# Two-layer cross-attention on one core: x and keys also loaded turned, their scalings spread over the partitions through DRAM, out0 and the residual left turned

## The reference, cut to what matters

```python
def layer0(x, c, f):                                   # out_a uses c, out_v uses f
    def cma(x, k):
        q = _ln(x) @ Wq + bq;  kk = _ln(k) @ Wk + bk;  v = _ln(k) @ Wv + bv
        return softmax(q @ kk.T * 128 ** -0.5) @ v @ Wo + bo
    res = cma(x, c) + cma(x, f) + x
    return _ln(res) @ fc_W + fc_b + res

def layer1(x1, c):
    Q = x1 @ Wq + bq;  K = c @ Wk + bk;  V = c @ Wv + bv
    return x1 + softmax(Q @ K.T * 128 ** -0.5) @ V @ Wo + bo
```

## Time and profile before

| | |
|---|---|
| time, median of 3 runs | 169.53 us (167.81 to 170.84) |
| profiled execution, first to last instruction | 167.2 us; the page lists no other time for it |
| TensorE busy | 155.5 us, 93% |
| VectorE busy | 131.4 us, 79% |
| ScalarE busy | 124.2 us, 74% |
| GpSimd busy | 76.4 us, 46% |
| moved by DMA | 15.93 MB |

### The profile page before, as it was taken

The page is one execution under the profiler, slowest core; times in us unless marked ns, Lnnn a source line. Parts: engine busy times, 40 slices in busy tenths (PEclk is TensorE's granted clock), DMA queues, the critical chain, the costliest instruction groups (busy, mean ns, idle before and its releaser), DMA issues.

```text
span 167.2 us, 6323 instructions
## 1 busy us (share of the span) xinstructions
PE 155.5 (93%) x2442; PEld 121.7 (73%) x2442; DVE 131.4 (79%) x400; ACT 124.2 (74%) x384; POOL 76.4 (46%) x104
## 2 busy tenths in 40 slices
PE   6799998999999999799999999989999999999682
PEld 6769674896689687767786787667788887995350
DVE  1693499999899789999999996497688997596531
ACT  3431559869988979599879788977978789866930
POOL 2026269789676523714979624194532022110210
PEclk9965579999999999999999999999999999999955
DMA  5999999900001010101010011001010100101113
GB/s 139 299 380 380 378 379 378 364 33 0 2 4 67 0 67 0 68 2 67 4 63 4 0 67 65 6 0 67 0 67 20 47 6 4 67 0 65 63 67 125
DMA packets 9982, 15.93 MB, mean 95 GB/s; under 512 B 1249, under 2 KB 3682, under 8 KB 9954
## 3 DMA queue, kind: packets, MB, share of 16 engines
q1 hardware_dynamic: 9522, 15.14, 25.1%
q10 hardware_dynamic: 432, 0.40, 1.0%
HBM read 11.35 MB, written 4.19 MB: 93 GB/s over the span
## 4 chain that ended last, share of the span: by engine, by line
PE 73%; DVE 9%; ACT 7%; issue 4%; DMA 3%; POOL 2%; ACTq 1%; POOLq 0%
PE ps L1526 9%; PE ps L1465 8%; PE ps L1508 7%; PE ps L1576 5%; PE ps L1516 5%; PE ps L1496 4%; PE ps L1541 4%; PE ps L1534 4%; PE ps L1485 4%; PE ps L1456 4%; PE ps L1475 4%; PE ps L1449 4%; DMA cf_sb<-in_cf 3%; PE ps L1568 3%; ACT exp L632 3%
## 5 line engine op out<-in xcount | busy, mean ns | idle before, releaser
L384 POOL TENSOR_TENSOR prob<-exp,rsum 128x512 f32<-128x512 f32 x16 | 16.7, 1042 | 23.5 <-DVE rsum L1025 23.5
L390 POOL TENSOR_TENSOR prob<-exp,rsum 128x256 f32<-128x256 f32 x16 | 9.8, 613 | 29.0 <-DVE rsum L1085 29.0
L356 POOL TENSOR_TENSOR z_sb<-x_sb,x_rstd 128x512 f32<-128x512 f32 x15 | 15.4, 1040 | 15.9 <-ACT x_rstd L543 14.1
L632 ACT ACTIVATE exp<-ps,exp_bias 128x64 f32<-128x64 f32 x64 | 19.2, 315 | 3.5 <-DVE exp_bias L1080 3.4
L1061 DVE SCALAR_TENSOR_TENSOR x_sb<-ps,res_rstd,res_sb 128x128 f32<-128x128 f32 x64 | 19.2, 342 | 0.2 <-issue 0.2
L1465 PE MATMUL ps<-zT_sb,m 128*128 128x512 f32 x32 | 17.8, 645 | 0.0
L1526 PE MATMUL ps<-wd,resT_sb 128*128 128x130 f32 x128 | 17.6, 280 | 0.0
L1508 PE MATMUL ps<-w,mix_sb 128*128 128x128 f32 x128 | 17.5, 280 | 0.0
L378 POOL TENSOR_TENSOR cfn_sb<-cf_scaled,cf_shift 128x512 f32<-128x512 f32 x15 | 15.6, 1042 | 4.0 <-issue 2.9
L1526 PEld LDWEIGHTS ps<-wd,resT_sb 128*128 128x128 f32 x128 | 15.6, 191 | 2.0 <-ACT resT_sb L609 1.5
L371 POOL TENSOR_TENSOR cf_scaled<-cf_sb,cf_rstd 128x512 f32<-128x512 f32 x15 | 15.4, 1043 | 2.7 <-ACT cf_rstd L555 2.5
(11 more groups left out here) (141 smaller groups left out, 384.2 us busy)
## 6 DMA issues: line engine op xcount, KB each, us to landing
x_sb<-in_x SPq DMA_DIRECT2D x16, 256.0 KB, 6.8
out<-out_sb SPq DMA_DIRECT2D x16, 256.0 KB, 2.0
cf_sb<-in_cf SPq DMA_DIRECT2D x15, 256.0 KB, 7.1
ct_sb<-in_ct SPq DMA_DIRECT2D x16, 128.0 KB, 7.9
...
cf_sb<-in_cf ACTq DMA_DIRECT2D x1, 256.0 KB, 4.9
...
```

Source lines behind the costliest of these rows:

```text
L356: pool.tensor_tensor(z_sb[:, g % Z_SLOTS, :, :], x_sb[:, g, :, :], wide_x(g), ALU.mult).then_inc(z_pool, 1)
L384: pool.tensor_tensor(prob0[:, g % PROB0_SLOTS, :, :, :], exp0[:, g % EXP0_SLOTS, :, :, :], wide0(rsum0, g), ALU.mult).then_inc(prob0_pool, 1)
L632: last = nc.scalar.activation(exp1[:, g % EXP1_SLOTS, p, :], ps[:, bank + u, v * S:(v + 1) * S], ACT.Exp, bias=exp1_bias[:, g, p:p + 1], a ...
```

## The change

- x is also loaded turned (xt: 128 features by 512 query columns) and, from group 4 on, both key sets too (kt). x, xt, cf, kt and ct no longer have a place for each group but 4, 8, 9, 3 and 6 slots, and SP waits for a slot to come free before it loads.
- Groups 0 to 3 (TURNED) still go by z, zT, copy_zT and cfT, copy_cfT. From group 4 on the scalings and shifts of a batch of two groups lie in 40 columns of `rows`; TensorE turns them (turn_rows), ScalarE copies them (copy_rowsT), SP stores them to DRAM (store_rows) and loads them back repeated over the partitions (spread_x, spread_k, spread_s, each 128 partitions by 1024 elements, 512 KB). GpSimd then multiplies or adds them (scale_xt, scale_kt, shift_kt), and t0 and s0 read the results. scale_cf stays for mix0, which now reads scaled keys without the shift.
- out0 is one matmul of 512 columns and its result is turned already. residual adds xt and a folded bias and writes resT_sb, which dense reads directly; resN turns it back for stats_res only, which reads PSUM. ScalarE scales dense's result (gain, four instructions), x1T turns it, x1 (VectorE) adds residual and bias in one instruction of 512 columns.
- The foldings of weights change a little (a bias as a column of the affine tile, bv and bo folded into out0's bias), `keep_busy` has 11 + 3 + 3 + 1 matmuls in place of 8, and the lists of all five engines are new.

```diff
-Z_SLOTS, ZT_SLOTS, CFS_SLOTS, CFN_SLOTS, CFT_SLOTS, T0_SLOTS, DIFF0_SLOTS = 3, 2, 2, 4, 2, 2, 2
-EXP0_SLOTS, PROB0_SLOTS, PROB0T_SLOTS, MIX0_SLOTS, RES_SLOTS, X1_SLOTS, REST_SLOTS = 2, 2, 2, 2, 4, 2, 2
+X_SLOTS, XT_SLOTS, CF_SLOTS, KT_SLOTS, CT_SLOTS, SPREAD_SLOTS = 4, 8, 9, 3, 6, 2
+Z_SLOTS, ZT_SLOTS, CFV_SLOTS, CFK_SLOTS, KS_SLOTS, CFT_SLOTS, T0_SLOTS, DIFF0_SLOTS = 2, 3, 4, 2, 2, 3, 2, 2
+EXP0_SLOTS, PROB0_SLOTS, PROB0T_SLOTS, MIX0_SLOTS, REST_SLOTS, GAIN_SLOTS = 2, 2, 2, 2, 4, 2
 X1T_SLOTS, T1_SLOTS, EXP1_SLOTS, PROB1_SLOTS, PROB1T_SLOTS, MIX1_SLOTS, OUT_SLOTS = 4, 2, 2, 2, 2, 2, 3
...
+TURNED = [0, 1, 2, 3]
+BATCHES = [[0], [1], [2, 3], [4, 5], [6, 7], [8, 9], [10, 11], [12, 13], [14, 15]]
+SPREAD_FROM = 3
...
+            def store_rows(b):
+                at = b - SPREAD_FROM
+                sp.wait_ge(rowsT_copied, at + 1)
+                sp.dma_start(rows_dram[at, :, :], rowsT[:, at % SPREAD_SLOTS, :]).then_inc(rows_stored[at % SPREAD_SLOTS], 16)
+
+            def spread_x(b):
+                at = b - SPREAD_FROM
+                sp.wait_ge(rows_stored[at % SPREAD_SLOTS], 16 * (at // SPREAD_SLOTS + 1))
+                if at >= SPREAD_SLOTS:
+                    sp.wait_ge(zT_scaled, BATCHES[b - SPREAD_SLOTS][-1] + 1 - len(TURNED))
+                sp.dma_start(x_spread[:, at % SPREAD_SLOTS, :, :].rearrange("p g t -> p (g t)"),
+                             rows_dram[at, 0:8, :].rearrange("r t -> (r t)").unsqueeze(0).broadcast_to([D, 8 * P])
+                             ).then_inc(x_spread_in[at % SPREAD_SLOTS], 16)
+
+            def spread_k(b):
+                at = b - SPREAD_FROM
+                sp.wait_ge(rows_stored[at % SPREAD_SLOTS], 16 * (at // SPREAD_SLOTS + 1))
+                if at >= SPREAD_SLOTS:
+                    sp.wait_ge(ks_done, BATCHES[b - SPREAD_SLOTS][-1] + 1 - len(TURNED))
+                sp.dma_start(k_spread[:, at % SPREAD_SLOTS, :, :].rearrange("p g t -> p (g t)"),
+                             rows_dram[at, 8:24, :].rearrange("(h r) t -> h (r t)", h=2).unsqueeze(1
+                             ).broadcast_to([2, C, 8 * P])).then_inc(k_spread_in[at % SPREAD_SLOTS], 16)
+
+            def spread_s(b):
+                at = b - SPREAD_FROM
+                sp.wait_ge(rows_stored[at % SPREAD_SLOTS], 16 * (at // SPREAD_SLOTS + 1))
+                if at >= SPREAD_SLOTS:
+                    sp.wait_ge(cfT_shifted, BATCHES[b - SPREAD_SLOTS][-1] + 1 - len(TURNED))
+                sp.dma_start(s_spread[:, at % SPREAD_SLOTS, :, :].rearrange("p g t -> p (g t)"),
+                             rows_dram[at, 24:40, :].rearrange("(h r) t -> h (r t)", h=2).unsqueeze(1
+                             ).broadcast_to([2, C, 8 * P])).then_inc(s_spread_in[at % SPREAD_SLOTS], 16)
...
+            def scale_xt(g):
+                slot, half = spread_at(g)
+                slot_in(pool, xt_in, g, XT_SLOTS)
+                spread_in(pool, x_spread_in, g)
+                need(pool, t0_made, g - ZT_SLOTS + 1)
+                pool.tensor_tensor(zT_sb[:, g % ZT_SLOTS, :], xt_sb[:, g % XT_SLOTS, :], x_spread[:, slot, half, :],
+                                   ALU.mult).then_inc(zT_scaled, 1)
+
+            def scale_kt(g):
+                slot, half = spread_at(g)
+                at = g - len(TURNED)
+                slot_in(pool, kt_in, g, KT_SLOTS, len(TURNED))
+                spread_in(pool, k_spread_in, g)
+                need(pool, cfT_shifted, at - KS_SLOTS + 1)
+                pool.tensor_tensor(blocks(ks_sb[:, g % KS_SLOTS, :]), kt_sb[:, at % KT_SLOTS, :, :, :, :],
+                                   blocks(k_spread[:, slot, half, :]), ALU.mult).then_inc(ks_done, 1)
+
+            def shift_kt(g):
+                slot, half = spread_at(g)
+                at = g - len(TURNED)
+                pool.wait_ge(ks_done, at + 1)
+                spread_in(pool, s_spread_in, g)
+                need(pool, s0_made, g - CFT_SLOTS + 1)
+                pool.tensor_tensor(cfT_sb[:, g % CFT_SLOTS, :, :, :, :], blocks(ks_sb[:, g % KS_SLOTS, :]),
+                                   blocks(s_spread[:, slot, half, :]), ALU.add).then_inc(cfT_shifted, 1)
...
+            def copy_rowsT(b, bank):
+                at = b - SPREAD_FROM
+                act.wait_ge(rowsT_made, at + 1)
+                if at >= SPREAD_SLOTS:
+                    act.wait_ge(rows_stored[at % SPREAD_SLOTS], 16 * (at // SPREAD_SLOTS))
+                nc.scalar.copy(rowsT[:, at % SPREAD_SLOTS, :], ps[0:40, bank, 0:P]).then_inc(rowsT_copied, 1)
...
-            def copy_resT(g, bank):
-                act.wait_ge(resT_made, g + 1)
-                need(act, dense_made, g - REST_SLOTS + 1)
-                nc.scalar.copy(resT_sb[:, g % REST_SLOTS, :], ps[:, bank, :]).then_inc(resT_copied, 1)
-
-            def copy_x1T(g, bank):
-                act.wait_ge(x1T_made, g + 1)
-                if g == 0:
-                    act.wait_ge(row_bias_done, 1)
-                need(act, final_done, g - X1T_SLOTS + 1)
-                nc.scalar.activation(x1T_sb[:, g % X1T_SLOTS, :], ps[:, bank, :], ACT.Identity, bias=row_bias[:, :]
-                                     ).then_inc(x1T_copied, 1)
+            def gain(g, bank):
+                act.wait_ge(dense_made, g + 1)
+                act.wait_ge(res_rstd_done, g + 1)
+                need(act, x1T_made, g - GAIN_SLOTS + 1)
+                for p in range(PAIRS):
+                    at = (p % 2) * (D + 2)
+                    last = nc.scalar.mul(gain_sb[:, g % GAIN_SLOTS, p, :], ps[:, bank + p // 2, at:at + D],
+                                         res_rstd[:, g, p // 2, p % 2:p % 2 + 1])
+                last.then_inc(gain_act, 1)
...
             def residual(g, bank):
                 dve.wait_ge(out0_made, g + 1)
-                need(dve, resT_made, g - RES_SLOTS + 1)
-                need(dve, x1_done, g - RES_SLOTS + 1)
-                v.tensor_tensor(res_sb[:, g % RES_SLOTS, :, :], by_pair(ps[:, bank, :]), x_sb[:, g, :, :], ALU.add
-                                ).then_inc(res_done, 1)
-
-            def stats_res(g):
-                dve.wait_ge(res_done, g + 1)
+                slot_in(dve, xt_in, g, XT_SLOTS)
+                if g == 0:
+                    dve.wait_ge(out0_bias_done, 1)
+                need(dve, resN_made, g - REST_SLOTS + 1)
+                need(dve, dense_made, g - REST_SLOTS + 1)
+                need(dve, x1T_done, g - REST_SLOTS + 1)
+                v.scalar_tensor_tensor(resT_sb[:, g % REST_SLOTS, :], ps[:, bank, :], out0_bias[:, 0:1],
+                                       xt_sb[:, g % XT_SLOTS, :], ALU.add, ALU.add).then_inc(res_done, 1)
+
+            def stats_res(g, bank):
+                dve.wait_ge(resN_made, g + 1)
                 for u in range(DUOS):
                     last = v.bn_stats(res_stats[:, g, u, :, :].rearrange("p v k -> p (v k)"),
-                                      res_sb[:, g % RES_SLOTS, 2 * u:2 * u + 2, :].rearrange("p v d -> p d v"))
+                                      ps[:, bank, 2 * u * P:2 * (u + 1) * P].rearrange("p (v d) -> p d v", v=2))
                 last.then_inc(res_stats_done, 1)
 
-            def x1(g, bank):
-                dve.wait_ge(dense_made, g + 1)
+            def key_biases(g, bank):
                 dve.wait_ge(res_rstd_done, g + 1)
-                need(dve, x1T_made, g - X1_SLOTS + 1)
...
+            def x1(g, bank):
+                dve.wait_ge(x1T_made, g + 1)
+                if g == 0:
+                    dve.wait_ge(row_bias_done, 1)
+                need(dve, t1_made, g - X1T_SLOTS + 1)
+                need(dve, final_done, g - X1T_SLOTS + 1)
+                v.scalar_tensor_tensor(x1T_sb[:, g % X1T_SLOTS, :], ps[:, bank, :], row_bias[:, 0:1],
+                                       resT_sb[:, g % REST_SLOTS, :], ALU.add, ALU.add).then_inc(x1T_done, 1)
 
...
+            def turn_rows(b, bank, *reads):
+                pe.wait_ge(x_rstd_done, b + 1)
+                pe.wait_ge(cf_shift_done, b + 1)
+                after(*reads)
+                nc.tensor.transpose(ps[0:40, bank, 0:P], rows[:, b, :], ident[:, :]).then_inc(rowsT_made, 1)
...
-                for u in range(DUOS):
-                    for v in range(2):
-                        p = 2 * u + v
-                        last = mm(ps[:, bank, p * P:(p + 1) * P], mix0_sb[:, g % MIX0_SLOTS, u, v, :, :], w01[:, 0:D],
-                                  start=True, stop=True)
-                last.then_inc(out0_made, 1)
-
-            def resT(g, bank, *reads):
+                mm(ps[:, bank, :], w01[:, 0:D], mix0_sb[:, g % MIX0_SLOTS, :, :, :, :], start=True, stop=True
+                   ).then_inc(out0_made, 1)
+
+            def resN(g, bank, *reads):
                 pe.wait_ge(res_done, g + 1)
                 after(*reads)
                 for p in range(PAIRS):
-                    last = nc.tensor.transpose(ps[:, bank, p * P:(p + 1) * P], res_sb[:, g % RES_SLOTS, p, :], ident[:, :])
```

(37 more changed lines are left out.)

1887 lines of the change are left out of this document (986 added, 901 removed).

## The result

The changed kernel takes **260.2 us**, median of four runs (257.6 to 261.6), against 169.7 us for the kernel before in four runs beside it: 1.533 times the time, 95% interval 1.517 to 1.548. The forecast was 248 us, from the case of two engines, whose own range was 226 to 272. Executions of one kernel can lie some per cent apart, so where the medians of two kernels are close their lowest runs are compared too. The profiled execution has a span of 259.3 us.

The account below looks back on a forecast made before the run. TensorE's instruction stream bounds the kernel before (93% of span); afterwards two DMA engines carrying the spreads: 35 + 132 + 8 + 18 + 12 + 2 + 5 + 34 = 246 us span, forecast 248 us, 8-in-10 range 163 to 272.

Parts of the forecast that it names:

- the case of two engines: spread_k and spread_s loads each move on only two of sixteen DMA engines: 248 us, own range 226 to 272, chance 0.70.
- The mechanism: In spread_k and spread_s, the source's slowest dimension counts 2, so two DMA engines each carry 256 KB and fourteen carry nothing.
- The size of a spread: One 512 KB spread_k or spread_s load on two engines at 23.75 GB/s each: 11.0 us, range 9.7 to 12.
- The low bound of 9.7 us: Shortest spread_k or spread_s load, its two engines undisturbed by the other fourteen; with all loads hidden, 226 us in total.
- The serial sum: Spreads and other loads queue on the two DMA engines as one serial resource: 246 us of span.
- the term of 12 us: Time the two DMA engines stand empty: waits at shifts(5) and store_rows(7), plus each batch's store and landing latency.
- TensorE: Its instruction stream: 13.4 us less transposes, 0.9 more small ones, 0.5 less out0, 1 more filler; 167.2 to 155.2 us.
- The other engines: Busy time of ScalarE 108 to 115 us, VectorE about 124, GpSimd 89, all beside TensorE and no bound.
- A: Rival: spreads go on many engines, round trip hidden, TensorE's saving holds: 159.5 us (153 to 164), chance 0.17.
- T: Length of one spread_k or spread_s load; a batch costs 2T + 1.4 + 5 us, fitting 15.9 us up to T = 4.7.
- B: Rival: many engines, but half the DRAM round trip shows, through SP's waits or late loads: 172 to 184 us, chance 0.13.
- the round trip of 8.5 us: A batch's scalings to DRAM and back with all sixteen engines sharing, inside 15.9 us of TensorE work per batch.

Follow-up runs that it names:

- The standalone loads: Separate SyncE-only kernel, one awaited 512 KB load at a time: source of 2 rows repeated 64 times 12.15 to 12.76 us, one row repeated 128 times 3.39 us.
- halves: Changed kernel with spread_k and spread_s each issued as two loads of one repeated row to 64 partitions: 173.9 us; run again 175.9 us, 1.029 times before.

## Why the prediction was right, step by step

**The mechanism** was the one named: the source's slowest dimension of two. It was argued from the code's two patterns and the durations of other transfers. The standalone loads (12.2 to 12.8 us against 3.4, with 0.13 of the engines busy) and halves (86 of 90 us) show it. GpSimd waited and TensorE was 62% busy, as said; but the DMA engines did not stay near 2/16 and 50 GB/s. In 40 to 60 and 100 to 120 us they were at 0.44 and 0.22, 134 and 75 GB/s, since the other loads run beside the spreads.

**The size of a spread** was taken as 11.0 us, and the first two are 10.9 us apart. The single one, waited for, is 12.2 to 12.8, which has the landing and the empty start in it. The low bound of 9.7 us has no row behind it; the quickest that two engines were seen to move is 51 GB/s, 10.3 us for 512 KB. The low end of the range does not come out of its own words either: 12 x 1.3 us less for the spreads and no 18 us for the loads give 248 - 34 = 214 us, not 226. The measured time lies at the other end, so nothing hung on it.

**The serial sum** was 35 + 132 + 8 + 18 + 12 + 2 + 5 + 34 = 246; the span is 259.3. The terms against the trace:

| term | predicted | in the trace |
|---|---|---|
| first spread issued | 35 | 30.8 |
| from there to the last landing | 172 | 187 (217.8 less 30.8) |
| from there to the end | 39 | 41.5 |

The first spread is 4 us early. The changed opening has the full clock from 10 to 20 us, and the kernel before with 14 filler matmuls shows that the filler brings 3.4 us of such a lead; it was priced at up to 4.8 us of cost and turned out a gain there. The chain of the kernel after has cfT(3) 4.6 us ahead of the earlier trace rows; the first out0 follows it:

```profile
26.33 0.59 PE ps L1679 x4
...
27.04 1.13 PE ps L1735 x2
```

The middle is the mis-sized step, by 15 us, and 11 of them lie in the term of 12 us for the time in which the two engines stand empty. The trace gives, from the use of a spread to the issue of the next: 85.0 to 91.7, 119.4 to 120.9, 149.4 to 162.3, and 190.5 to 192.6, 23 us in all, bounded by when GpSimd could use the landed rows. The longest is at the batch that the prediction named: k_spread(6) is used at 149.44, and store_rows(7) goes out at 158.58, 9.1 us later. But the way there is another. The prediction had store_rows(7) stand behind load_kt(13), which needs scale_kt(10); load_kt(13) went out at 150.72 already. The rows themselves came late: shifts(7) stands in GpSimd's list behind scale_kt(10) and (11), three other kinds of work and shift_kt(10), and runs at 156.70, though ScalarE's part of its inputs was there at 151.5; then come TensorE's turn at 157.97 and ScalarE's copy at 158.29. The prediction had named this kind of wait for shifts(5) and did not count it for batch 7. So of the sum the term for the empty engines was mis-sized, 12 us for 23, by the GpSimd work that stands between a landing and the next rows. That GpSimd work is a likely part of what made the kernel with one two-engine load a batch slower than expected, too.

**TensorE.** Four groups are still turned, 16 transposes each of zT and cfT. Where the long waits are gone, TensorE is busy for 146.8 us (halves) and 144.0 us (without the later spreads; 145.8 in its second run), 9 to 12 us under before; predicted were 12 less (155.2 against 167.2 of span). Part of it is the clock of the opening: before with 14 filler matmuls has 152.9 us, 2.6 less than before. The filler takes 6.7 us in halves in place of 3.8, by its groups. out0 takes 0.86 us in the chain of halves, as priced.

**The other engines**, from the groups of the kernel after (columns as in the earlier trace rows):

```profile
L566 POOL TENSOR_TENSOR ks_sb<-kt_sb,k_spread 128x512 f32<-128x512 f32 x12 | 15.1, 1266 | 64.2 <-DMA k_spread<-rows_dram 34.9
...
L1270 DVE SCALAR_TENSOR_TENSOR x1T_sb<-ps,row_bias,resT_sb 128x512 f32<-128x512 f32 x16 | 11.9, 744 | 29.8 <-PE ps L1761 29.5
...
L581 POOL TENSOR_TENSOR prob<-exp,rsum 128x512 f32<-128x512 f32 x16 | 16.8, 1047 | 7.9 <-DVE rsum L1223 7.9
...
L836 ACT ACTIVATE gain_sb<-ps,res_rstd 128x128 f32<-128x128 f32 x64 | 18.3, 374 | 1.4 <-PE ps L1753 0.4
```

ScalarE's scalings are 18.3 us in all, predicted 17.9, with 114.2 us for the engine (108 to 115). VectorE's 125.2 meets the 124; x1 is 744 ns in place of 686. GpSimd is under-priced: a multiplication of two full tiles takes 1.27 us, the one with a row's factor repeated along it 1.05, and the price had been read from the latter. Thirty-six of them make 8 of the 9 us between 98.4 and the 89 forecast. Little of this was on the path that sets the end.

**The rivals.** A failed on its condition, since T was two engines. What A needs was run as halves, with T of at most 2.6 us where A holds up to 4.7, and A's 159.5 us did not come: 174 to 176. The size is B's (172 to 184). B gave two reasons, SyncE held at a wait for the round trip, or the three full loads of a batch landing late. With the round trip taken away and the loads kept the time stayed, so the first is not it; the second is what is left. What A had too low is the round trip of 8.5 us inside a budget of 15.9, which counts a spread at 1.4 us of an otherwise free DMA. A batch of halves has three spreads of 1.7 to 2.2 us at the rates measured and its ordinary loads, which now include the turned x and keys; the engines are 0.91 busy from 40 to 60 us, and an x_spread lands 6.8 us after its issue in the median. Only where the later spreads are left out does TensorE's saving reach the end, 163 to 165 us.

**What stays open.** How the halves' 24 us above TensorE's busy time divide between single waits is not settled: late x and cf loads (4.6 and 3.8 us of VectorE's waits), GpSimd's waits for the spreads (8.5 us for k, 4.4 for s) and TensorE's for zT (7.3 us) overlap, and none was removed alone. Nor is it known what the spreads would cost if they were issued earlier, with more slots for them. And no version of this change beat the kernel before with the whole computation done.
